# Loading the second FFN weight matrix in single 128-row tiles instead of pairs, each load waiting for its own buffer

## What is computed

```
def _L0_ffn_ref(x, w1, b1, w2, b2):
    def _binarize(w):
        alpha = mean(abs(w), axis=1, keepdims=True)
        return alpha * sign(w)            # forward value
    h = einsum('bsd,hd->bsh', x, _binarize(w1)) + b1
    h = gelu(h, approximate=False)
    out = einsum('bsh,dh->bsd', h, _binarize(w2)) + b2
# layer 0: x = x + attention(layernorm(x)) + ffn(layernorm(x))
# layer 1: x = x + rotor attention(layernorm(x)) + tree ffn(layernorm(x))
```

## Time and profile before

| | us |
|---|---|
| median of 2 runs | 3938.06 |
| lowest and highest run | 3935.64, 3940.49 |
| the profiled execution | 3957.53 |
| its span on the slowest core (core 4) | 3956.0 |
| PE busy in the span | 2982.2 (75%) |
| DVE, ACT busy | 1438.2, 939.4 |

### The profile page before, as it was taken

The page is one execution under the profiler, slowest core; times in us unless marked ns, Lnnn a source line. Parts: engine busy times, 40 slices in busy tenths (PEclk is TensorE's granted clock), DMA queues, the critical chain, the costliest instruction groups (busy, mean ns, idle before and its releaser), DMA issues.

```text
span 3956.0 us, 41127 instructions; the slowest of 8 cores (3904.2 to 3956.0 us)
## 1 busy us (share of the span) xinstructions
PE 2982.2 (75%) x14368; PEld 1353.8 (34%) x14368; DVE 1438.2 (36%) x1387; ACT 939.4 (24%) x1061; POOL 92.1 (2%) x173
## 2 busy tenths in 40 slices
PE   2398999999999436999999996243313737998997
PEld 1143444444444202444444442221101312333333
DVE  7213233333333100000000002789996214544443
ACT  5232222222222375111222221521100002111220
POOL 0000000000000000000000000100000010000000
PEclk9998899999999757999999998576656968999999
DMA  4611111111111352111111112620013881111112
GB/s 144 165 54 28 33 33 33 33 33 42 33 33 33 85 86 42 54 54 54 43 36 40 43 54 81 172 68 21 22 32 120 272 186 35 66 67 61 64 43 75
DMA packets 136936, 264.14 MB, mean 67 GB/s; under 512 B 41488, under 2 KB 82720, under 8 KB 134688
## 3 DMA queue, kind: packets, MB, share of 16 engines
q1 hardware_dynamic: 114624, 194.89, 16.7%
q0 software_dynamic: 22112, 66.63, 7.3%
HBM read 202.22 MB, written 92.29 MB: 74 GB/s over the span
## 4 chain that ended last, share of the span: by engine, by line
PE 64%; DVE 19%; DMA 8%; ACT 4%; issue 4%; DVEq 0%; SPq 0%; ACTq 0%; POOL 0%; PEldq 0%; POOLq 0%; PEld 0%
PE c_pe L581 11%; PE d_pO L938 11%; PE d_pH L925 11%; PE c_pO L612 9%; PE g_pO L1378 6%; PE g_pL L1411 5%; PE c_pO L621 3%; PE b_pf L503 3%; DVE f_Pc L214 2%; DMA f_rbT<-rC_h 2%; DVE f_tmp L214 2%; DVE f_Qc L214 2%; PE f_pO L1282 2%; DVE e_st L214 1%; DVE f_cos L214 1%
## 5 line engine op out<-in xcount | busy, mean ns | idle before, releaser
L581 PE MATMUL c_pe<-fC 128*128 128x512 bf16 x2048 | 463.9, 389 | 10.7 <-ACT e_sb L680 7.6
L938 PE MATMUL d_pO<-sw2T,d_hC 128*128 128x512 bf16 x2048 | 443.3, 379 | 9.4 <-ACT d_hC L214 9.4
L925 PE MATMUL d_pH<-d_xc,sw1T 128*128 128x512 bf16 x2048 | 445.6, 380 | 1.9 <-DVE d_a2bc L214 1.8
L214 ACT ACT_TABLE_LOAD x86 | 110.3, 1283 | 1157.8 <-PE g_pL L1411 377.0
L612 PE MATMUL c_pO<-fT,aT_sb 128*128 128x512 bf16 x1536 | 357.6, 387 | 31.9 <-ACT aT_sb L668 31.9
L214 ACT ACTIVATE d_hC<-d_pH,b_col_sb,d_a1col 128x512 bf16<-128x512 f32 x256 | 199.1, 778 | 637.6 <-PE d_pH L925 637.5
L1411 PE MATMUL g_pL<-g_xc,WinTb 128*128 128x512 bf16 x1216 | 278.3, 386 | 88.0 <-DMA g_xc<-xn1C_h 64.3
L971 DVE TENSOR_TENSOR d_x1o<-d_pO,d_a2bc 128x1024 f32<-128x1024 f32 x32 | 39.2, 1224 | 818.8 <-PE d_pO L938 818.8
L581 PEld LDWEIGHTS c_pe<-fC 128*128 128x128 bf16 x2048 | 203.9, 100 | 265.2 <-issue 58.6
L938 PEld LDWEIGHTS d_pO<-sw2T,d_hC 128*128 128x128 bf16 x2048 | 199.8, 98 | 252.9 <-issue 13.2
L1140 PE MATMUL f_pV<-xn1C,Wvo 128*128 128x512 bf16 x512 | 125.6, 411 | 213.2 <-ACT f_v L214 180.4
(11 more groups left out here) (116 smaller groups left out, 2590.1 us busy)
## 6 DMA issues: line engine op xcount, KB each, us to landing
c_xr<-x SPq DMA_DIRECT2D x32, 512.0 KB, 4.9
x1p_h<-c_x1p SPq DMA_DIRECT2D x32, 512.0 KB, 5.7
d_x1p<-x1p_h SPq DMA_DIRECT2D x32, 512.0 KB, 4.3
x_h<-d_x1o SPq DMA_DIRECT2D x32, 512.0 KB, 5.2
f_x1r<-x_h SPq DMA_DIRECT2D x32, 512.0 KB, 5.7
x2p_h<-f_x2p SPq DMA_DIRECT2D x32, 512.0 KB, 6.7
g_x2p<-x2p_h SPq DMA_DIRECT2D x32, 512.0 KB, 4.0
out<-g_out POOLq DMA_DIRECT2D x32, 512.0 KB, 4.6
```

What stands on the lines that cost most here:

```text
L214: ins = f(*a, **k)
L581: ins = tensor.matmul(pe_[:, (r % 2) * 512:(r % 2 + 1) * 512], fC[:, k * T + s * 128:k * T + (s + 1) * 128], fC[:, k * T + q * 512:k * T + ...
L925: ins = tensor.matmul(pH[:, (r % 2) * 512:(r % 2 + 1) * 512], sw1T[:, k * T + jt * 128:k * T + (jt + 1) * 128], xchunk[:, xoff + k * 512:x ...
L938: ins = tensor.matmul(pO[:, (i % 2) * 1024 + dc * 512:(i % 2) * 1024 + (dc + 1) * 512], hC[:, jt * 512 + sub * 128:jt * 512 + (sub + 1) * ...
```

## The change

The w2 tiles are loaded one by one. 16 DMAs of two tiles become 32 DMAs of one. The load of tile jt now waits for the ones-matmul of tile jt-4, whose slot it takes, and of no later tile. ACT waits for the load of its own tile. The bytes, the slots, the work of ACT, PE and DVE, and the four semaphores stay.

```diff
-        for pq in range(NTT // 2):
-            jt = 2 * pq
+        for jt in range(NTT):
             r = NKT + jt
             if jt < 4:
                 gpsimd.wait_ge(TE.h, NKT * NCH)
             else:
-                gpsimd.wait_ge(TE.h, NKT * NCH + (jt - 2) * 2)
-            LW.issue(gpsimd.dma_start(
-                out=wraw[:, (r % 4) * T:(r % 4 + 2) * T].rearrange(
-                    "p (s c) -> p s c", s=2)[:, :, 0:1024],
-                in_=dw2T[jt * 128:(jt + 2) * 128, :].rearrange(
-                    "(s p) c -> p s c", p=128)))
+                gpsimd.wait_ge(TE.h, NKT * NCH + (jt - 3) * 2)
+            LW.issue(gpsimd.dma_start(out=wraw[:, (r % 4) * T:(r % 4) * T + 1024],
+                                      in_=dw2T[jt * 128:(jt + 1) * 128, :]))
...
-            LW.wait_done(scalar, NKT // 2 + jt // 2)
+            LW.wait_done(scalar, NKT // 2 + jt)
```

## The result

The changed kernel takes 0.9921 of the time of the kernel before, 95% interval [0.9885, 0.9956]: about 31 us less, with 17 to 45 in the interval. It took 3909.48 to 3915.59 us. Some executions of these kernels run slower, at a lower granted clock on one die (cores 0 to 3 or 4 to 7) or both (4305 us in one of the changed kernel, with 0.81 on cores 0 to 3 and 0.90 on the others): no time or ratio here contains them, and where a profile is such an execution, the text takes the cores of the other die and names them.

What follows compares the result with a forecast made beforehand. The w2 preparation was taken as bound by ACT with load waits through four slots. Gains of 17.05 and 1.3 less 0.7 us gave 17.7 us, so 3920.4 us from 3938.06, range 3904 to 3940.

Steps and rivals of the forecast that it cites:

- What bounds the stretch: w2 preparation before the feed-forward: ACT and its load waits set the path, so any shortening there shortens the kernel.
- The steady state: w2 loop through four slots: ACT's recurring load gaps vanish if a landing is at most 5.15 us; gain 17.05 us.
- The supply: w2 loads: 1.28 us of transfer a tile against ACT's 2.30 us, queue used to 56%, so DMA keeps up.
- serial service: Rival on w2 loads: fixed parts don't overlap, 4.0 to 4.1 us a tile, time 3976 us; chance 0.04.
- The start: First w2 load to ACT's first Sign: a single tile lands sooner than a pair; gain 1.3 us, bounds 0 to 2.2.
- The end: Before the first feed-forward matmul: a1col comes last, so 0.7 us of gain is not won; bounds 0 to 2.0.
- the landing L of a single: Time from a single w2 load's issue to its landing: taken as 4.0 us, bounds 3.9 and 5.17.
- The sum: Whole kernel: 17.05 + 1.3 - 0.7 = 17.7 us won, taken off the median 3938.06, giving 3920.4 us.
- Longer landings: Rival on w2 loads: landings stretch to 6.8 us, 2.71 us a tile, time 3933 us; chance 0.08.
- Given back: Rival: the stretch's gain vanishes in the time, through the a1 chain or execution differences; 3930 to 3942 us; chance 0.08.

Runs made afterwards that it cites:

- again: The changed kernel measured once more, unaltered, beside the kernel before: ratio 0.9949 [0.9932, 0.9966].
- pairwait: Changed kernel, but each single load waits for the second tile of the pair two before, as the pairs did; its single execution took 3934.33 us.
- deeppairs: Kernel before with pairs kept, but w2 tiles packed into sixteen slots, eight pairs loaded ahead; ratio to the kernel before 0.9962 [0.9946, 0.9978].
- double: Changed kernel with a further, unused load of the same tile ahead of each w2 load, ACT waiting for both; its single execution took 3951.48 us.
- best2: best with both a1 DMAs moved back behind the last w2 load; ratio to the kernel before 0.9853 [0.9801, 0.9905].
- best: Changed kernel with sixteen w2 slots, w2 loads begun during w1, absolute values on DVE, single w1 loads, a1 DMAs amid w2's; 0.9846 of the kernel before.
- bestpairs: best with the w2 loads in pairs, half as many DMAs for the same bytes; its executions took 3871.74 and 3873.80 us.
- a1early: Changed kernel with the a1 store after w2 load 3 and its load back after load 7; no ratio, three parts sum to 83.6 us instead of 82.2.

## Why the prediction was right, and where it was not

**What bounds the stretch.** Right. ACT, then a loop through four slots; the stretch lies on the path, and what it gets shorter the cores get shorter (mean span 3928.2 to 3906.8 us in again, 21 us).

**The steady state.** Predicted 17.05 us, measured 18.4 in the mean of the cores (89.96 to 71.55), and 16.9 from core 4 before (88.2) to core 4 after (71.3), the core on which the sum was made. The other cores of before waited more often, up to 15 times, and most of them longer in sum, up to 30.7 us. The condition, a landing under 5.15 us, held in the median (4.7) but not in each load (13% took longer, up to 8.0 us); that left up to 1.1 us of gaps on a core. The landing of 4.0 us was too low: the term hardly hung on it, as the prediction said. pairwait and deeppairs confirm the mechanism from both sides.

**The supply.** The verdict was right and the number too good. 1.28 us a load is the rate of the best slices of WoT's stream, and the best distance of two landings in this stage; the mean with a full queue is 1.6 us (double). WoT's own eight loads land 1.57 us apart on core 4 and 1.49 us in the mean of the cores, and the paragraph on serial service had 1.56 us from the same rows. The margin was 2.30 against 1.6, not against 1.28. The waits of the even tiles became earlier by a whole tile of the loop, 2.30 us, where the prediction says one matmul.

**The start.** 1.3 us predicted, 1.6 measured (5.5 to 3.9).

**The end.** The right resource, the wrong size. a1col does come last now, and costs 1.5 us instead of 0.7. The failed step is that the store "would be behind one tile, which is 1.28 us less": the issue of a1col follows that of the store after 4.9 us (1471.92 - 1467.05) on core 5 and 3.8 to 5.5 on the others, where it was 5.1 to 5.8 and I expected 3.8. In the mean that is 4.9 instead of 5.4 us, so 0.5 us less and not 1.28. That the store hangs on the load ahead of it was right: by the landing times it lands 0.2 us after that load on every core, before the change and after it, and in best2 too, where that is 17 us and more after its issue. The size was wrong: the last pair landed 5.4 us after its issue and the last single 4.7, not 4.0, and as the single is issued 0.2 us faster, 0.5 us are left. So it is the landing L of a single that was mis-sized, and here, unlike in the steady state, the sum hangs on it. The a1col load landed after 6.3 us in the mean (up to 7.2), near the 6.4 taken. PE starts 1.9 us after the end of a2bc in the mean, where 1.0 was expected. The upper bound of 2.0 us held in the mean; core 2 with an end of 7.5 us lost 2.4.

**The sum.** 17.7 predicted; 18.5 by the traces; 20 us (13 to 27) by the second comparison; 31 (17 to 45) by the first. That the change is worth the same in each execution was right, and that the median of before can be taken as the base too. The time was 3920 predicted and 3912 us measured (median). The repeat has 3921.27 in its median, so the 8 us are of the size of the scatter of executions, of which the prediction had allowed 16. That the time came within 8 us is in part luck: the scatter is nearly as large as the gain. Three slips in its sums change nothing: 32 x 2.30 is 73.6, and the 73.4 that it uses belongs to the 2.295 us between the Signs of rows 5; 18.2 less 11.4 is 6.8; and the last gap is 2.3 us by rows 9, not 2.35.

**The rivals.** Serial service is refuted (double: 1.6 us a load). With it goes the estimate of 2.6 us as a service time for each single, which the prediction made from the fit in the Trainium skill, "DMA: Bandwidth & Descriptors", section "Anatomy of one DMA — SWDGE (gpsimd) path". The same page's section "Rules for kernel authors" asks for 1 MiB loads for the most bandwidth, and here single loads of 256 KB in four slots took as long as pairs of 512 KB in sixteen (82.2 and 82.4 us): what bound this loop was the landing, and not the bandwidth. Longer landings: partly true, 4.7 instead of 4.0 us, with at most 1.1 us of gaps on a core. Given back: 1.5 us, at a1col.

## What to carry to other kernels
Draw a staging buffer as a loop: free, wait, issue, landing, use; divide its length by the number of slots, and compare that with the time that the consumer takes for a slot. If it is longer, smaller loads, an earlier wait and more slots all help, and the last is often free when a slot is larger than what is in it, as here, where packing gave sixteen slots for four. Once the loop is covered, look for the wait that was hidden behind it (here a chain of two small DMAs), and move such a chain only where the loads queued behind it have slack.

## What the runs showed of the hardware that was not expected
- Queued loads of one kind (128 x 1024 float32 to bf16 from POOL) often landed 1.25 us apart, which is 210 GB/s, at the output projection's weights and at w2 alike. The mean was 1.49 us for the former (before, all cores) and 1.6 us in double, 1.40 us in best. What makes the difference is open. Pairs took 1.39 us a tile (bestpairs), so between 256 and 512 KB the size of the DMA plays no part.
- The w2 load right behind a load of 4096 single 4-byte values landed after 7.6 to 9.6 us (a1early, cores 4 to 7), where the median of the changed kernel is 4.7, late enough for ACT to wait 1.95 to 2.69 us.
- POOL's issue took 0.53 us for a single and 0.71 for a pair. A small store lands 0.2 us after the w2 load that is queued ahead of it: after 3.2 to 4.9 us in the changed kernel, after 17.0 to 20.7 us behind the last burst of w2 loads (best2). Only in a1early it is 0.2 to 0.7 us.
